# One block for the first attention and the search, tables among the key stores, key loads behind the first gathered rows, first scores as two, three, three

## The chip, the cores and the metric

The kernel runs on one core of a Trainium2 chip. The metric is the device time of one execution in microseconds (us); lower is better. A core has engines that run their own instruction streams and meet only at semaphores: TensorE (PE; its weight loads are shown as PEld), VectorE (DVE), ScalarE (ACT), GpSimd (POOL) and SyncE (SP), which here does nothing but start transfers. Transfers started by any of them run on the core's 16 DMA engines. In the profile an engine name with a q at its end (SPq, PEq, POOLq) is that engine's instruction queue: DMA starts, branches and barriers are put down to it.

## The reference

Two layers over x (16 batches, 112 tokens, width 256), each of them a cross attention to ctx (16 batches, 375 rows) and a feed-forward part. The first attention has no softmax; the first feed-forward is expert choice: each of 8 experts takes the 224 of the 1792 tokens with its highest gate scores. The second attention is an ordinary softmax attention with 16 heads, the second feed-forward a mixture with LoRA parts.

```python
# layer 0: x = x + attention(layernorm(x), ctx) without softmax, with its own layernorm
score = jnp.einsum('bhqd,bhkd->bhqk', Q, K) / dk
attn = jnp.where(mask, -jnp.inf, score)
...
# layer 0, feed-forward
k = int(bs * CAPACITY) // n
scores = jax.nn.softmax(xf @ gate_w.T, axis=-1)
vals, idx = jax.lax.top_k(scores.T, k)
...
h = jax.nn.gelu(h, approximate=True)
out = jnp.einsum('knf,ndf->knd', h, fc2s) + b2s
out = out * kept_w[..., None]
xf = xf.at[flat_idx].add(out.reshape(k * n, d))
...
# layer 1: x = x + softmax attention(layernorm(x), ctx), then the LoRA mixture
K = (key_value @ Wk.T + bk).reshape(B, SKV, H, Dh).transpose(0, 2, 1, 3)
weights = jax.nn.softmax(scores, axis=-1)
```

## The kernel before

The work is laid out in stages, each engine's part written as one function per block (`nc.Block`); a block ends with a barrier of all engines.

**Block 1, 0 to 170 us: the first attention.** It goes over 8 pairs of batches. The tail of a pair (`tail`, parts 0 to 6 on VectorE) adds the attention's result to x, normalises three times and gives `x1`, `xin` (the gate's input) and `z`. TensorE turns `xin` and multiplies it with the gate's weights (`gate_turn`, `gate_product`), ScalarE copies both (`gate_inputs`, `gate_logits`). GpSimd's `powers` raises the variances to -0.5 and, in its third step, adds `total` = x1 + xin. SyncE stores `z` to `gath_d`, from which the experts gather, and `total` to `sum_d`. Behind the last pair's products TensorE has already done 10 of 64 key pieces of the second attention (`key_piece`, L182; a piece is two matmuls on ctx and `wk1`, and a batch has four pieces).

**Block 2, 171.5 to 225 us: the gate and the search.** VectorE makes the softmax of the gate: the maximum (L872), `shifted` (L875), ScalarE's Exp into `raised` (L795), the sum (L878) and the scores. Then come 16 rounds (`bits`) that find for each expert the score that 224 tokens reach, two bits at a time: VectorE writes candidates and `above` (L920), TensorE counts (`tally`, L828), VectorE reduces the count (L925) and takes the bits. Between the tallies TensorE does the other key pieces, 3 or 4 in a round. Each batch's keys are kept as three bfloat16 parts in `kp`, which has KEPT = 5 slots: the first part is ScalarE's copy (L791, two for a batch), the whole value is `kf` (L798), the remainders `kr` are VectorE's `remainder(n)` (L895, one half, in round n, queued between `above` and the reduction of the count) and GpSimd's `second_half(n)` (L772), ScalarE copies them as second part (L807), GpSimd subtracts the third (L780). SyncE stores the three parts to `kparts_d` (L761), at most two stores under way; ScalarE waits for the store of batch n - 5 before it writes batch n. At the head of SyncE's part of the block stand three tables for the experts: `iota`, `b1` and `b2` (L753). In rounds 0 to 3 VectorE also splits the scores in three parts (`score_parts`, L901 to L910) for `find`.

After the last round VectorE writes `gt_eq_q` (L948) and, by way of two more products of TensorE, `pos1`, the place of each token in its expert's list. TensorE does values of the second attention in between (`value`, L730).

**Block 3, from 225 us: the experts.** For each expert `find` (one-hot rows against `token5`, L1070 and L1131) gives the indices, GpSimd gathers the expert's 224 rows of `gath_d` in two indirect transfers (L1038), TensorE turns them (L1141), multiplies (L1154 and, behind gelu, L1169) and GpSimd adds the weighted result to `sum_d` (L1047). The indices of expert e + 2 and their gathers are made during expert e. SyncE begins this block with the key loads of the first three batches (`load_keys`, L744: nine transfers from `kparts_d` to `kpk`) and then loads the weights `we` of experts 2 to 7, each when the expert two before is done (L997). Values of the second attention fill TensorE up to the first turn (L1141 at 241.3).

**Block 4, from 368 us: the second attention.** Statistics of x (`statistics`), `normal(i)` (L1888, VectorE), the turn of `xn` (L2047) and the queries (L2057) go pair by pair; their parts are copied as for the keys, with `remainder(i)` on VectorE (L1897). From pair 4 on TensorE does the scores of batch 0 in between (`score`, L2075, 8 groups, listed by pair in `FIRST_SCORES`), and VectorE takes their row maxima (`two_max`, L1920). `shift_turn(0)` (L2084) turns the maxima; ScalarE spreads the shift (L1809), TensorE forms the transposed scores (L2100), ScalarE their exponentials (`probs`, L1828). The stretch from there to about 600 us is 16 such steps; then the last feed-forward runs to the end.

## Time and profile before

| | us |
|---|---|
| median of 3 runs | 766.07 |
| lowest, highest | 765.29, 771.0 |
| the profiled execution | 770.76 |
| its span (first to last instruction) | 768.9 |
| mean granted TensorE clock, share of full | 0.978 |
| busy: TensorE, VectorE, ScalarE, GpSimd | 715.1, 501.3, 336.8, 293.9 |

The profile is taken from one execution. Its times count from the start of the span, so a row that begins with 171.52 starts 171.52 us into it. A group of instructions stands as one row: its start, the time from its first start to its last end, the engine, the line of the kernel, the operation, what it writes and reads, their shapes and how many instructions there are. In brackets at the end of a row stands how long the engine had been idle before it, and behind the arrow what ended this. PEclk is the clock that TensorE was granted, as a share of 2.4 GHz; at 0.50 it is 1.2 GHz.

### The profile page before, as it was taken

The page shows a single profiled execution, that of the slowest core. Times are in us where ns is not written, and L with a number is a line of the kernel's source. Part 1 is how long each engine was busy: PE and PEld are TensorE (multiplying, and loading weights), DVE is VectorE, ACT ScalarE, POOL GpSimd, SP SyncE. Part 2 cuts the span into 40 slices and gives each one's busy share as a digit, 9 for nine tenths or more (in the row PEclk, how much of TensorE's full clock was granted, in tenths as well). Part 3 has the DMA queues.
Part 4 walks back from the last instruction along what each step waited for, and adds up shares of the span by engine and source line. Part 5 has one row for each costly group of instructions (what it writes and reads, how often), then busy time and mean ns, then how long its engine had stood idle before and what let it go on. Part 6 is the DMA issues. An engine that isn't in the chain of part 4 may idle for free. (4 is left out here: it accounts for less than half of the span.)

```text
span 768.9 us, 16709 instructions
## 1 busy us (share of the span) xinstructions
PE 715.1 (93%) x6469; PEld 608.4 (79%) x6469; DVE 501.3 (65%) x1263; ACT 336.8 (44%) x689; POOL 293.9 (38%) x222
## 2 busy tenths in 40 slices
PE   4899999979988999999987999999998898999998
PEld 3678788855577989898875778777776787898998
DVE  4688888878862322320367787878788777767565
ACT  2112222218733221222546787777777642423323
POOL 2233333428841232232432877778778200000000
PEclk9999999999998999999998999999999999999999
DMA  9978000017889444543534588877762000000001
GB/s 295 336 225 50 25 25 25 26 49 206 196 176 159 133 147 134 147 164 89 108 94 92 115 149 164 172 150 155 148 142 37 2 2 13 1 25 1 25 5 34
DMA packets 65611, 81.55 MB, mean 106 GB/s; under 512 B 32018, under 2 KB 55154, under 8 KB 64226
## 3 DMA queue, kind: packets, MB, share of 16 engines
q1 hardware_dynamic: 62306, 72.22, 39.7%
q0 software_dynamic: 2816, 3.67, 2.7%
q10 hardware_dynamic: 416, 4.65, 1.6%
q8 instruction: 50, 0.82, 0.5%
q14 instruction: 23, 0.19, 0.1%
HBM read 60.45 MB, written 19.31 MB: 104 GB/s over the span
## 5 line engine op out<-in xcount | busy, mean ns | idle before, releaser
L1920 DVE TENSOR_REDUCE mx<-psum 112x2 f32<-112x750 f32 x128 | 113.2, 926 | 14.1 <-PE psum L2075 13.6
L1828 ACT ACTIVATE probs<-psum 125x448 f32<-125x448 f32 x192 | 91.1, 545 | 28.9 <-PE psum L2100 28.5
L574 PE MATMUL psum<-w_parts,c_parts 128*125 128x512 f32 x288 | 74.5, 412 | 11.0 <-DVE w_parts L437 10.6
L1735 POOL TENSOR_TENSOR half_sum<-probs 125x896 f32<-125x896 f32 x30 | 62.7, 2089 | 42.9 <-ACT probs L1828 42.8
L2100 PEld LDWEIGHTS psum<-qpk,kpk 128*125 128x125 bf16 x768 | 62.4, 141 | 15.3 <-issue 8.0
L574 PEld LDWEIGHTS psum<-w_parts,c_parts 128*125 128x125 f32 x288 | 54.2, 192 | 25.1 <-DVE w_parts L437 10.6
L2100 PE MATMUL psum<-qpk,kpk 128*125 128x112 bf16 x768 | 67.9, 227 | 2.6 <-ACT probs L1828 2.1
L2075 PE MATMUL psum<-kpk,qpk 96*112 96x375 bf16 x256 | 63.5, 342 | 6.3 <-DVE mx L1920 4.9
L1741 POOL TENSOR_TENSOR tile_sum<-half_sum,probs 125x896 f32<-125x896 f32 x30 | 62.5, 2084 | 3.4 <-issue 1.1
L1169 PE MATMUL psum<-we,hT 128*112 128x256 f32 x256 | 59.7, 394 | 0.0
L1014 ACT ACTIVATE hT<-psum,b 128x224 f32<-128x224 f32 x64 | 25.1, 443 | 78.8 <-PE psum L1154 78.8
L1440 ACT ACTIVATE ctx_all<-psum,cols 128x448 f32<-128x448 f32 (+1 forms) x40 | 22.4, 560 | 81.5 <-PE psum L1606 81.5
L1169 PEld LDWEIGHTS psum<-we,hT 128*112 128x112 f32 x256 | 46.9, 185 | 10.5
L1154 PE MATMUL psum<-rT,we 128*128 128x224 f32 x256 | 52.1, 364 | 0.9 <-ACT rT L1005 0.9
L1154 PEld LDWEIGHTS psum<-rT,we 128*128 128x128 f32 x256 | 50.2, 197 | 2.1 <-issue 1.2
L185 PE MATMUL psum<-ctx_all,wk 128*128 128x375 f32 x128 | 46.3, 504 | 3.6 <-PEq L264 3.5
L1101 DVE TENSOR_TENSOR tmp<-psum,b 112x512 f32<-112x512 f32 x8 | 5.5, 692 | 67.6 <-PE psum L1169 67.6
L2413 PE MATMUL psum<-wo_parts,hs_parts 128*112 128x256 f32 x384 | 48.1, 281 | 1.0 <-DVE hs_parts L2311 0.9
L2413 PEld LDWEIGHTS psum<-wo_parts,hs_parts 128*112 128x112 f32 x384 | 46.1, 175 | 1.9 <-DVE hs_parts L2311 1.6
L1047 POOL DMA_INDIRECT sum_d<-outs,idx_add x16 | 23.8, 1490 | 61.4 <-DVE outs L1105 37.0
L1412 POOL TENSOR_TENSOR rs<-ve,mhalf 112x4 f32<-112x4 f32 (+1 forms) x5 | 4.9, 975 | 109.2 <-DVE ve L1455 109.2
L1552 DVE SCALAR_TENSOR_TENSOR ctx_all<-psum,neg_bi,ctx_all 128x448 f32<-128x448 f32 (+1 forms) x40 | 23.5, 589 | 34.4 <-PE psum L1619 33.9
(234 smaller groups left out, 1498.7 us busy)
## 6 DMA issues: line engine op xcount, KB each, us to landing
we<-in_we SPq DMA_DIRECT2D x6, 2048.0 KB, 9.1
kparts_d<-kp SPq DMA_DIRECT2D x16, 562.5 KB, 5.3
kpk<-kparts_d SPq DMA_DIRECT2D x16, 562.5 KB, 6.2
ctx_all<-in_ctxT SPq DMA_DIRECT2D x16, 375.0 KB, 6.0
kpk<-kparts_d SPq DMA_DIRECT2D x16, 375.0 KB, 7.0
we<-in_we ACTq DMA_DIRECT2D x2, 2048.0 KB, 13.3
kpk<-kparts_d SPq DMA_DIRECT2D x16, 187.5 KB, 4.0
qparts_d<-qp SPq DMA_DIRECT2D x16, 168.0 KB, 3.1
```

The lines of the kernel that those rows point to most:

```text
L185: ins = pe.matmul(k_bank(n, m)[:, 0:SK], wk1[:, k, m * 128:(m + 1) * 128], ctx_of(n)[:, k], start=(k == 0), stop=(k == KC - 1))
L574: ins = pe.matmul(banks[B_KV[t]][0:KT, :], parts_of[:, x, k, t * KT:(t + 1) * KT], w_parts[:, k, w], start=(k == 0 and (x, w) == SPLIT[0]) ...
L1014: ins = act.activation(hT[:, s, f], banks[B_F[g]][:, (f % 2) * CAP:(f % 2 + 1) * CAP], ACT.Gelu_apprx_tanh, bias=b1[:, e, f:f + 1])
L1154: ins = pe.matmul(banks[B_F[g]][:, (f % 2) * CAP:(f % 2 + 1) * CAP], we1[:, s, k, f * 128:(f + 1) * 128], rT[:, s, k], start=(k == 0), sto ...
L1169: ins = pe.matmul(banks[B_OUT[s]][0:SQ, h * D:(h + 1) * D], hT[:, s, f, h * SQ:(h + 1) * SQ], we2[:, s, f], start=(f == 0), stop=(f == FC ...
L1735: pool.tensor_tensor(half_sum[:, m], probs[:, m, 0], probs[:, m, 1], ALU.add)\
L1741: pool.tensor_tensor(tile_sum[:, m], half_sum[:, m], probs[:, m, 2], ALU.add)\
L1828: act.activation(probs[:, m, t, g * HU * SQ:(g + 1) * HU * SQ], banks[B_ST[u % 3]][0:KT, 0:HU * SQ], ACT.Exp, scale=SCALE)\
L1920: dve.tensor_reduce(mx[:, n % 2, H + 2 * j:H + 2 * j + 2], psum[0:SQ, first:first + 2, 0:SK], AX.X, ALU.max)\
L2075: ins = pe.matmul(banks[B_S[j % 2] + h][0:SQ, 0:SK], qpk[0:ROWS, s, 2 * j + h], kpk[0:ROWS, s, 2 * j + h], start=True, stop=True)
L2100: ins = pe.matmul(banks[B_ST[u % 3]][0:KT, c * SQ:(c + 1) * SQ], kpk[:, s, h, t * KT:(t + 1) * KT], qpk[:, s, h], start=True, stop=True)
L2413: ins = pe.matmul(y_of(i, s), hs_parts[:, x, f, s * SQ:(s + 1) * SQ], wo_parts[:, w, f], start=(f == 0 and (x, w) == SPLIT[0]), stop=(f == ...
```

## The change

Four things are changed.

1. The functions of block 1 are written into block 2, so that the barrier between them goes. With it the order at the seam changes on each engine. VectorE makes the gate's maximum and `shifted` before the last pair's `z`, and `remainder(0)` moves into that pair's tail; `remainder(1)` and `(2)` come a round earlier and `remainder(15)` behind `gt_eq_q`. ScalarE copies the keys of batches 0 and 1 before the gate's input and logits. GpSimd's sum of the last pair moves behind the first tally. The four operations on the score parts leave VectorE: two are now ScalarE's copies, two GpSimd's subtractions. `shifted` and `raised` lie in PSUM.
2. The tables go among the key stores: `iota`, `b1` and half of `b2` behind the seventh store, the other half of `b2` behind the tenth.
3. SyncE's key loads wait until the rows of experts 0 and 1 have landed.
4. At the second attention's entry `FIRST_SCORES` is two, three, three; `normal` runs three pairs ahead, the statistics and the powers of all later pairs are done at pair 0, and `shift_turn(0)` waits for the last turned `xn` but one and not for the last query remainder.

The core of the diff (moved functions that are the same before and after are left out):

```diff
-FIRST_SCORES = {4: (0, 1), 5: (2, 3), 6: (4, 5), 7: (6, 7)}
+FIRST_SCORES = {4: (0, 1), 5: (2, 3, 4), 6: (5, 6, 7)}
...
-        with nc.Block() as block:
-            @block.sync
...
 (SyncE)
-        for dst, name in ((iota, "c_iota"), (b1, "b1"), (b2, "b2")):
-            sp.dma_start(dst[:], d[name]).then_inc(tabs_in.sem, 16)
+        sp.wait_ge(lg_done.sem, lg_done.at(PAIRS - 1))
         for n in range(B):
+            if n == 7:
+                for dst, name in ((iota, "c_iota"), (b1, "b1")):
+                    sp.dma_start(dst[:], d[name]).then_inc(tabs_in.sem, 16)
+            if n in (7, 10):
+                half = slice(0, E0 // 2) if n == 7 else slice(E0 // 2, E0)
+                sp.dma_start(b2[:, half], d["b2"][:, half]).then_inc(tabs_in.sem, 16)
...
 (ScalarE)
-                gate_inputs(PAIRS - 1)
-                gate_logits(PAIRS - 1)
-        first_part(0)
+        act.wait_ge(x1_done.sem, x1_done.at(PAIRS - 1))
+        first_parts(0)
+        whole(0)
+        first_parts(1)
+        gate_inputs(PAIRS - 1)
+        whole(1)
+        gate_logits(PAIRS - 1)
+        act.wait_ge(max_off.sem, max_off.at(0))
+        act.activation(raised[:], shifted[:], ACT.Exp).then_inc(exp_done.sem, 1)
+        act.wait_ge(z_done.sem, z_done.at(PAIRS - 1))
+        first_parts(2)
...
+            if n == 1:
+                act.wait_ge(count_done.sem, count_done.at(0))
+                act.activation(token5[:, :, 2], scores[:].rearrange("p b e -> p (b e)"), ACT.Copy)\
+                    .then_inc(parts_done.sem, 1)
+            if n == 6:
+                act.wait_ge(parts_done.sem, 2)
+                act.activation(token5[:, :, 3], rest[:], ACT.Copy).then_inc(parts_done.sem, 1)
...
 (GpSimd)
         second_half(0)
+        pool.wait_ge(count_done.sem, count_done.at(0))
         for n in range(B):
+            if n == 1:
+                sums(PAIRS - 1)
             if n + 1 < B:
                 second_half(n + 1)
...
+            if n == 3:
+                pool.wait_ge(parts_done.sem, 1)
+                pool.tensor_tensor(rest[:], scores[:].rearrange("p b e -> p (b e)"), token5[:, :, 2], ALU.subtract)\
+                    .then_inc(parts_done.sem, 1)
+            if n == 8:
+                pool.wait_ge(parts_done.sem, 3)
+                pool.tensor_tensor(token5[:, :, 4], rest[:], token5[:, :, 3], ALU.subtract).then_inc(parts_done.sem, 1)
...
 (VectorE)
+        for part in range(2 * NKT):
+            if part == 4:
+                remainder(0)
+            tail(part, PAIRS - 1, 1, more=False)
+
         route.step(0)
 
+        dve.wait_ge(lg_done.sem, lg_done.at(PAIRS - 1))
         dve.tensor_reduce(small[:, 0], logits[:], AX.X, ALU.max).then_inc(route.next(), 1)
         dve.memset(cur, 0.0)
         dve.wait_ge(route.sem, route.count())
         dve.tensor_tensor(shifted[:], logits[:], spread(small[:, 0], 2, E0), ALU.subtract)\
             .then_inc(max_off.sem, 1)
+        tail(2 * NKT, PAIRS - 1, 1, more=False)
...
+        remainder_at = lambda n: n - 1 if n < 3 else n
...
-            remainder(r)
-            score_parts(r)
+            for n in range(1, B - 1):
+                if remainder_at(n) == r:
+                    remainder(n)
...
         ins.then_inc(gt_eq_q_done.sem, 1)
+        remainder(B - 1)
...
 (the experts' block, SyncE, then TensorE)
+        for s in range(2):
+            sp.wait_ge(gathered[s].sem, gathered[s].at(0))
         for b in range(AHEAD):
             for r in (3, 2, 1):
                 load_keys(sp, b, r)
...
+        pe.wait_ge(parts_done.sem, 4)
         find(0, 0)
...
 (the second attention: GpSimd, VectorE, TensorE)
-            if i + STATS_AHEAD < PAIRS:
-                power(i + STATS_AHEAD)
+            if i == 0:
+                for later in range(STATS_AHEAD, PAIRS):
+                    power(later)
...
-            if i + 2 < PAIRS:
-                normal(i + 2)
+            if i + 3 < PAIRS:
+                normal(i + 3)
+            scored = FIRST_SCORES.get(i, ())
+            ahead = int(len(scored) > 2)
+            for j in scored[:ahead]:
+                two_max(0, j)
             remainder(i)
-            if i + STATS_AHEAD < PAIRS:
-                statistics(i + STATS_AHEAD)
-            for j in FIRST_SCORES.get(i, ()):
+            if i == 0:
+                for later in range(STATS_AHEAD, PAIRS):
+                    statistics(later)
+            for j in scored[ahead:]:
                 two_max(0, j)
...
-        pe.wait_ge(qr_done.sem, qr_done.at(PAIRS - 1))
+        pe.wait_ge(xnT_done.sem, xnT_done.at(PAIRS - 2))
         shift_turn(0)
         for j in range(2):
             score(1, j)
+        pe.wait_ge(qr_done.sem, qr_done.at(PAIRS - 1))
```

The next rows are VectorE's instructions in order, from the last pair's third variance to the sum of the softmax; first before, then after the change. A row has the line, the operation, the tile written and those read, the shape, and the semaphores it waits for.

```order
L483 TENSOR_SCALAR ve<-mv 112x2 [waits stats]
L533 SCALAR_TENSOR_TENSOR t<-xin,mv,rows 112x256 x2
L543 SCALAR_TENSOR_TENSOR z<-t,rs,rows 112x256 [waits z_out,rstd_done,stats]
L543 SCALAR_TENSOR_TENSOR z<-t,rs,rows 112x256
L264 UNCONDITIONAL_BRANCH
L867 UNCONDITIONAL_BRANCH [waits barrier_Pool_Activation_PE_DVE_SP_release]
L872 TENSOR_REDUCE small<-logits 112x16
L873 MEMSET psum 112x8
L875 TENSOR_TENSOR shifted<-logits,small 112x128 [waits route]
L878 TENSOR_REDUCE small<-raised 112x16 [waits exp_done]
```

```order
L669 TENSOR_SCALAR ve<-mv 112x2 [waits stats]
L727 SCALAR_TENSOR_TENSOR t<-xin,mv,rows 112x256 x2
L761 TENSOR_REDUCE small<-logits 112x16 [waits lg_done]
L762 MEMSET psum 112x8
L764 TENSOR_TENSOR psum<-logits,small 112x128 [waits route]
L737 SCALAR_TENSOR_TENSOR z<-t,rs,rows 112x256 [waits z_out,rstd_done,stats]
L737 SCALAR_TENSOR_TENSOR z<-t,rs,rows 112x256
L768 TENSOR_REDUCE small<-psum 112x16 [waits exp_done]
```

The branches of the block's end and the wait for the barrier are gone, and the maximum and the subtraction stand ahead of the two `z` operations, behind which the Exp's result is waited for.

SyncE's order in the search and at the head of the experts' block, after the change (`k_out0` and `k_out1` are the landings of earlier stores, `gathered0` and `gathered1` those of the first two experts' rows). Before it, the three tables `iota`, `b` (`b1`) and `b` (`b2`, 112x2048 in one) stood ahead of the first store.

```order
L412 DMA kparts_d<-kp 128x6x375 [waits k3_done,k_out0,k2_done,k1_done]
L402 DMA iota<-in_c_iota 112x224
L402 DMA b<-in_b 128x64
L405 DMA b<-in_b 112x1024
L412 DMA kparts_d<-kp 128x6x375 [waits k3_done,k_out1,k2_done,k1_done]
L412 DMA kparts_d<-kp 128x6x375 [waits k3_done,k_out0,k2_done,k1_done]
L412 DMA kparts_d<-kp 128x6x375 [waits k3_done,k_out1,k2_done,k1_done]
L405 DMA b<-in_b 112x1024
...
L1004 UNCONDITIONAL_BRANCH [waits k_out1,k_out0]
L356 DMA kpk<-kparts_d 48x2x3000 [waits gathered1,gathered0]
```

Four transfers now stand between stores that wait for one another, and the first key load has a wait of its own.

TensorE's order from the scores behind pair 5's queries to the first shift turn, before and after (L2057 and L2082 are the queries, L2075 and L2100 the scores, two rows for one group; L2084 and L2109 the turn of the maxima).

```order
L2075 MATMUL psum<-kpk,qpk 112x375 [waits max_done]
L2075 MATMUL psum<-kpk,qpk 112x375
L2057 MATMUL psum<-xnT,wq 128x224 [waits qr_done,xnT_done]
L2057 MATMUL psum<-xnT,wq 128x224 x3
L2075 MATMUL psum<-kpk,qpk 112x375 [waits max_done]
L2075 MATMUL psum<-kpk,qpk 112x375
L2075 MATMUL psum<-kpk,qpk 112x375 [waits max_done]
L2075 MATMUL psum<-kpk,qpk 112x375
L2084 MATMUL psum<-ident,mx 32x112 [waits max_done,qr_done]
```

```order
L2100 MATMUL psum<-kpk,qpk 112x375 [waits max_done]
L2100 MATMUL psum<-kpk,qpk 112x375
L2100 MATMUL psum<-kpk,qpk 112x375 [waits max_done]
L2100 MATMUL psum<-kpk,qpk 112x375
L2082 MATMUL psum<-xnT,wq 128x224 [waits qr_done,xnT_done]
L2082 MATMUL psum<-xnT,wq 128x224 x3
L2109 MATMUL psum<-ident,mx 32x112 [waits max_done,xnT_done]
```

The last pair's queries are no longer followed by two groups of scores, and the turn behind them waits for `xnT_done` where it waited for `qr_done`.

## Rows read from the trace of the kernel before

**Rows 1.** The page, part 1: busy us (share of the span) and instructions.

```profile
PE 715.1 (93%) x6469; PEld 608.4 (79%) x6469; DVE 501.3 (65%) x1263; ACT 336.8 (44%) x689; POOL 293.9 (38%) x222
```

**Rows 2.** Windows: span, busy us by engine, then PEclk, DMA share, GB/s.

```profile
190.00:200.00 10.00, 10.00 (x48) 5.85 (x48) 8.24 (x29) 8.12 (x16) 8.72 (x9) 1.00 0.84 193
200.00:210.00 10.00, 10.00 (x50) 5.90 (x48) 7.93 (x28) 7.34 (x14) 8.68 (x7) 1.00 0.77 187
210.00:220.00 10.00, 8.86 (x67) 6.77 (x66) 5.62 (x20) 5.42 (x9) 6.30 (x6) 1.00 0.98 225
310.00:320.00 10.00, 10.00 (x65) 8.78 (x64) 2.93 (x17) 2.90 (x7) 3.97 (x4) 0.83 0.63 206
```

**Rows 3.** The timeline at the block boundary: start, us, engine, line, operation.

```profile
156.12 0.87 DVE L543 SCALAR_TENSOR_TENSOR z<-t,rs,rows 112x256 f32<-112x256 f32 x2
...
168.11 1.25 POOL L385 TENSOR_TENSOR total<-x,xin 112x512 f32<-112x512 f32 x1
168.20 0.18 ACT L345 ACTIVATE logits<-psum 112x16 f32<-112x16 f32 x1 [1.04 <-PE psum L639]
168.23 1.82 DVE L543 SCALAR_TENSOR_TENSOR z<-t,rs,rows 112x256 f32<-112x256 f32 x2 [0.25 <-DVE t L533]
...
171.52 0.29 DVE L872 TENSOR_REDUCE small<-logits 112x16 f32<-112x128 f32 x1 [1.47 <-PEq L264]
...
172.51 0.29 DVE L878 TENSOR_REDUCE small<-raised 112x16 f32<-112x128 f32 x1 [0.37 <-ACT raised L795]
...
174.30 0.31 PE L828 MATMUL psum<-above,ones 112*128 112x32 bf16 x4
...
174.71 3.45 PE L185 MATMUL psum<-ctx_all,wk 128*128 128x375 f32 x8
...
185.31 2.76 PE L185 MATMUL psum<-ctx_all,wk 128*128 128x375 f32 x8
```

**Rows 4.** The timeline of TensorE before and in the first experts.

```profile
231.39 7.15 PE L730 MATMUL psum<-wv,ctx_all 128*125 128x256 f32 x32
241.29 1.01 PE L1141 MATMUL psum<-ident,rows 112*128 112x112 f32 x4 [2.74 <-DMA rows<-gath_d,idx]
243.19 8.54 PE L1154 MATMUL psum<-rT,we 128*128 128x224 f32 x32 [0.90 <-ACT rT L1005]
...
268.24 0.58 PE L1141 MATMUL psum<-ident,rows 112*128 112x112 f32 x4
...
275.56 6.22 PE L1154 MATMUL psum<-rT,we 128*128 128x224 f32 x32
```

**Rows 5.** Waits in 395 to 420 us, before and in the first scores.

```profile
PE psum L2047 <- DVE xn L1888: 3.7, 2, 2.2
```

**Rows 6.** The timeline at the first shift and first probabilities.

```profile
417.94 0.54 PE L2084 MATMUL psum<-ident,mx 112*32 112x112 f32 x4 [1.97 <-DVE mx L1920]
...
421.64 2.37 ACT L1828 ACTIVATE probs<-psum 125x448 f32<-125x448 f32 x5
```

**Rows 7.** The timeline at the last round of the search.

```profile
212.37 0.34 PE L828 MATMUL psum<-above,ones 112*128 112x96 bf16 x4 [0.34 <-DVE above L920]
...
213.32 0.61 DVE L895 SCALAR_TENSOR_TENSOR kr<-psum,cols,kp 128x375 f32<-128x375 f32 x1 [1.00 <-POOL kp L780]
...
213.84 0.26 DVE L925 TENSOR_REDUCE psum<-psum 112x24 f32<-112x96 f32 x1
```

**Rows 8.** Issues in 170 to 262 us: KB of one, us to landing.

```profile
kparts_d<-kp SPq DMA_DIRECT2D x16, 562.5 KB, 5.3
...
b<-in_b SPq DMA_DIRECT2D x1, 896.0 KB
```

**Rows 9.** Issues in 228 to 230 us: key loads and a gather.

```profile
kpk<-kparts_d SPq DMA_DIRECT2D x1, 562.5 KB, 18.4
...
rows<-gath_d,idx POOLq DMA_INDIRECT x2, 12.4
```

**Rows 10.** Issues in 254 to 257 us: two gathers, no key load.

```profile
rows<-gath_d,idx POOLq DMA_INDIRECT x2, 2.8
```

879 lines of the change are left out of this document (430 added, 449 removed).

## The prediction

> **What bounds the kernel now.** I read four views in this order. The page first: TensorE is busy 93% of the span [rows 1], so a gain has to come out of the 7% in which it idles, or out of stretches in which it runs at half clock. The busy shares by window next: in the search (190 to 210 us) TensorE is full, VectorE has 8 of 10 us and GpSimd 8.7, and the DMA engines are at 0.84 and 0.77, then 0.98 in 210 to 220 [rows 2]. That stretch is a chain over five engines, not TensorE alone. Then the timeline around the three places that the change touches. At the block boundary VectorE has the gate's logits at 168.38 (168.20 + 0.18) and first looks at them at 171.52 [rows 3]. Before the first expert TensorE ends its values at 238.54 (231.39 + 7.15), idles 2.74 us for gathered rows, and then runs the turn and the first product slowly: 1.01 and 8.54 us, where the same groups take 0.58 and 6.22 later [rows 4]. Before the first scores of the second attention it idles 3.7 us in two waits for `xn` and 1.97 us for the last row maximum [rows 5, 6]. The expert loop behind it keeps TensorE full, 10.00 of 10 in the window shown [rows 2], so what is saved before it arrives at its end.
>
> **Part A, one block.** The barrier goes, and VectorE runs the maximum and `shifted` ahead of `z`, so that ScalarE's Exp lies under `z`. VectorE can start the maximum at 168.40. From the start of the maximum to the first tally took 2.78 us (171.52 to 174.30), 0.37 of it waiting for Exp [rows 3]. Add `z` at its normal 0.87 and take the 0.37 out: the tally comes at 168.40 + 2.78 + 0.87 - 0.37 = 171.68, or 2.6 us earlier. `z` took 1.82 before, beside GpSimd's sum of 1.25; another pair's took 0.87 [rows 3], and the change moves this sum behind the first tally. That is the 0.95 in the gain that has least to do with the barrier; if `z` stays slow the gain is 1.6. The upper bound is from the clock: eight key matmuls took 3.45 us at 174.71, after the idle at the barrier, and 2.76 at 185.31 [rows 3]. TensorE now has key pieces to do where it stood idle, and if its clock stays at 2.4 GHz, 0.7 more is saved, together 3.3. I take 2.6. The copies of the first two batches' keys and remainder(0) move ahead into waits for GpSimd and cost nothing: TensorE's order has the pieces that they need ahead of the last pair's turn, as before.
>
> The GpSimd half that now runs at 168.14 stands beside `shifted`. The Trainium skill, "SBUF — State Buffer", in its single rule on contention says that a VectorE instruction with two SBUF inputs and a GpSimd one reading SBUF exclude each other for the whole instruction; by that `shifted` would start some 0.3 us late and the term would be 2.3. The doubled `z` beside the sum agrees with it.
>
> **Part A, the last round.** VectorE waited 1.00 us for GpSimd, then ran a remainder of 0.61, and reduced at 213.84 a count that TensorE had begun at 212.37 and ended at 212.71 [rows 7]. The remainder is now behind `gt_eq_q`. The reduction could start at about 212.85: 1.0 us. The four score-part operations leave VectorE too, but in rounds that TensorE or the chain bounds; nothing for them. Two of them and the sum are new on GpSimd, which has 1.3 us free in ten [rows 2]: 1.25 for the sum and between 0.2 and 1.25 for each subtraction, some 2 to 3 us in a search of 40. They can make the keys late, not the tallies, until a kept buffer is missing.
>
> **Part B, tables among the stores.** 896 KB [rows 8] and 81 KB of small tables leave the stretch in which no store was waiting, and go among the stores behind the seventh and tenth (about 193 and 203 us before). At the 193 to 225 GB/s of those windows they take 4.3 to 5.1 us of the DMA engines, say 4.7. Idle there between 193.6 and 210 is 0.16 x 6.4 + 0.23 x 10 = 3.3 us [rows 2]; the 1.4 left over goes into 210 to 220, where the share is 0.98, so the late stores slip by it. A store frees one of five buffers, ScalarE's next copy waits for it, VectorE's remainder for that, and the count's reduction is queued behind the remainder. I take 1.3 given back; below it nothing (the rounds have their own slack), above it all 4.7. **A and B: 2.6 + 1.0 - 1.3 = 2.3 us**, between -1.1 (1.6 + 1.0 - 3.7, where one us of the 4.7 falls in the rounds' slack) and 4.3.
>
> **Part C, key loads behind the first rows.** Nine key loads (3.4 MB) went out at 225 and the gathers were issued among them. A gather landed 12.4 us later [rows 9]; with no key load beside it one takes 2.8 [rows 10]. Expert 0's second gather left at 228.56 and landed at 241.3, when the turn began. Now it leaves with the engines free: 228.56 - 2.3 + 2.8 = 229.1, expert 1's at about 234.1, and the values end at 236.2. The wait goes: 2.74. With it the half clock should go, since TensorE idles only the 0.90 for `rT`: 1.01 - 0.58 = 0.43 and 8.54 - 6.22 = 2.32 [rows 4]. **C: 5.5 us.** If the clock falls anyway, 2.7. What is late next: SyncE issues the key loads from 234.1 on, they end about 20 us later (one took 18.4 [rows 9]), so near 254. The gathers of expert 2, at 254 to 256 before, now leave near 246.7 and 248, beside them. At 12.4 us they land at 260.4 at the latest; the turn that needs them was at 268.24 [rows 4] and comes at 260.4. So the margin is nought by that figure and several us if the last key load's end sets it. Keys themselves aren't needed before 400.
>
> The Trainium skill, "DMA: Bandwidth & Descriptors", section "Queues, rings and completion order", speaks against this part: each DMA engine takes turns between queue rows, packet by packet. GpSimd's gather has a row of its own, so beside one queue of key loads it would take about twice 2.8, 5.6 us, and land before the values end with or without the change; C would be nothing. The 12.4 us doesn't agree with that.
>
> **Part D, entry of the second attention.** `normal` goes one pair further ahead, maxima come two, three, three, the first shift turns after them and no longer after the last query remainder. Waits of 3.7 for `xn` and 1.97 at the turn can go [rows 5, 6]. But the first probabilities, at 421.64, stand at the end of ScalarE's chain (query parts of the last pair, table load, values, spread), and that chain keeps its work; it starts earlier only as the last pair's queries do. The five pairs' copies still alternate between TensorE, ScalarE and VectorE. **I take 1.0**, between 0 and the whole 5.7, nearer to 0, as the ScalarE chain isn't shortened.
>
> **Sum.** 2.3 + 5.5 + 1.0 = 8.8 us, that is 770.76 - 8.8 = 762.0 against the profiled execution (span 768.9, 1.9 around it). That execution lies 4.7 above the median of the runs shown, 766.07. The gain is in waits that each execution has, so the median goes to 766.07 - 8.8 = 757.3; half-clock spells fall differently in other executions, and I say 757.5. One per cent (7.66 us) is about what a measurement of this kernel can tell from no change; 758.4 is that bound.
>
> **Rivals.**
> 1. The clock falls again between values and first expert (it fell under the same low activity before). C is 2.7, the sum 6.0: 760.1. Chance 0.17.
> 2. The stores give the search's gain back whole (GpSimd and DMA both near full for it, the extra slack of TensorE's rounds against): A and B are 0: 6.5 stay, 759.6. At the lower end, 1.1 lost, it is 760.7. Chance 0.13.
> 3. C doesn't do what it says: late key loads hold expert 2's gathers or the expert weights behind them on SyncE's queue, or the gather was slow from something else. 8.8 - 5.5 = 3.3: 762.8. For it speaks the margin of nought, against it that all key loads are out by 254. Chance 0.10.
> 4. The scores' order pays all of D's waits (5.7) and no other term changes: 13.5, 752.6. Chance 0.12.
> 5. Slower than before: the half clock. Two of the eight experts had a spell in the find and turn, where the matmuls are small though TensorE is full; each cost 10 x (1 - 0.83) = 1.7 us [rows 2]. With the loop 8 us earlier all eight could be hit: 6 x 1.7 = 10.2, more than 8.8: 767.5. It decides from five further spells on. Against it: six of eight passed before. Chance 0.05.
>
> The forecast has the remaining 0.43, with a range of its own of 755.5 to 760. Faster by over 1%: most of it and rival 4, 0.5. Within 1%: 0.45. Slower: 0.05. The range 752.5 to 764 leaves out rival 5, and the worst of 2 and 3 together.
>
> **What would show it.** Tally at 171.7 or earlier, `z` 0.87; reduction of the last round right behind its tally; first find near 221.4. No TensorE wait for rows before the first turn, products of 6.2 us, rows landing in about 3 us. Expert loop 7 to 8 us earlier, its end too. First probabilities at 412.5 to 413. I would be wrong if ScalarE's waits for stores grow beyond 1.5 us each, if the turn of expert 2 waits for rows, or if more than two spells of half clock stand in the expert loop.

## The result

Measured side by side with the kernel before, the changed kernel takes 765.93 us (median of 20 runs, 762.98 to 767.69) against 768.85 (20 runs, 765.29 to 771.37). The ratio is 0.9967, with a 95% interval of 0.9952 to 0.9983: 2.5 us or 0.3% faster, where 8.6 us (757.5, range 752.5 to 764) was forecast. The base of the forecast, 766.07, was the median of three runs; twenty runs of the same kernel gave 768.85, so 2.8 of the 8.4 us between 757.5 and 765.93 lie in the base and not in what the change did. The profiled executions differ by 3.2 us: 765.7 us of span against 768.9. Most of what is missing was given back in three places that the sum didn't contain: the values ahead of the experts, the choice of the tokens, and the expert loop.

The page of the changed kernel, part 1 and the span (columns as in [rows 1]):

```profile
span 765.7 us, 16706 instructions
...
PE 715.2 (93%) x6469; PEld 608.3 (79%) x6469; DVE 500.9 (65%) x1259; ACT 337.8 (44%) x691; POOL 294.9 (39%) x224
```

TensorE's busy time is the same to 0.1 us (715.1 in [rows 1]); the half clock stretches busy time, so this alone doesn't show what it did. The timeline of the changed kernel at the place where the barrier was, which answers to [rows 3]:

```profile
166.36 2.13 DVE L727 SCALAR_TENSOR_TENSOR t<-xin,mv,rows 112x256 f32<-112x256 f32 x2
...
167.37 0.84 POOL L574 TENSOR_TENSOR kr<-kf,kp 128x375 f32<-128x375 f32 x1
...
168.41 0.27 DVE L761 TENSOR_REDUCE small<-logits 112x16 f32<-112x128 f32 x1
...
168.93 0.87 DVE L737 SCALAR_TENSOR_TENSOR z<-t,rs,rows 112x256 f32<-112x256 f32 x2
...
169.72 0.28 DVE L768 TENSOR_REDUCE small<-psum 112x16 f32<-112x128 f32 x1
...
171.49 0.25 PE L950 MATMUL psum<-above,ones 112*128 112x32 bf16 x4 [2.27 <-DVE above L789]
...
171.59 4.46 PE L185 MATMUL psum<-ctx_all,wk 128*128 128x375 f32 x8
```

`z` is back at 0.87, as forecast, and the sum starts 1.31 us behind the maximum's start. But now the `t` operations before it take 2.13 us and not 0.88 as in the kernel before:

```profile
167.10 0.88 DVE L533 SCALAR_TENSOR_TENSOR t<-xin,mv,rows 112x256 f32<-112x256 f32 x2
```

The first key remainder of GpSimd (0.84) lies beside them, where `powers` and then the sum stood before. The first tally is at 171.49, 2.8 us earlier; 0.75 of this came up in the first 82 us, which the change doesn't touch, so the part's own share is 2.06. Behind it eight key matmuls take 4.46 us where they took 3.45 [rows 3]: the clock falls later here, to 1.2 GHz about 0.9 us behind the start of the first tally (granted clock 1.00 in 171.49 to 172.40, 0.51 in 172.40 to 175.89).

The last round and the choice of the tokens, which answer to [rows 7]:

```profile
210.68 0.34 PE L950 MATMUL psum<-above,ones 112*128 112x96 bf16 x4 [0.65 <-DVE above L789]
...
211.06 0.27 DVE L795 TENSOR_REDUCE psum<-psum 112x24 f32<-112x96 f32 x1 [0.44 <-PE psum L950]
...
214.18 3.14 POOL L585 TENSOR_TENSOR kp<-kr,kp 128x750 bf16<-128x750 f32 x2
...
214.62 1.28 DVE L832 TENSOR_TENSOR tie<-tie,gt_eq_q 112x128 f32<-112x128 f32 x1
...
215.93 1.54 DVE L834 TENSOR_TENSOR taken<-tie,gt_eq_q 112x128 bf16<-112x128 f32 x1
```

The reduction now starts 0.38 behind its tally, 1.47 before; that is the microsecond that the moved remainder was to bring. Then `tie` and `taken` take 1.28 and 1.54 us beside two key parts of GpSimd (3.14 together). In the trace of the kernel before they took 0.29 each, since they came after GpSimd had ended (214.24 + 3.08 = 217.32); only `need` ahead of them took 0.55 there, 0.17 here. These are the rows of the kernel before:

```profile
214.24 3.08 POOL L780 TENSOR_TENSOR kp<-kr,kp 128x750 bf16<-128x750 f32 x2
...
217.70 0.29 DVE L962 TENSOR_TENSOR tie<-tie,gt_eq_q 112x128 f32<-112x128 f32 x1
218.03 0.29 DVE L964 TENSOR_TENSOR taken<-tie,gt_eq_q 112x128 bf16<-112x128 f32 x1
```

The first experts, which answer to [rows 4], and the gathers, which answer to [rows 9, 10]:

```profile
230.07 8.84 PE L342 MATMUL psum<-wv,ctx_all 128*125 128x256 f32 x32
238.74 0.55 PE L1158 MATMUL psum<-ident,rows 112*128 112x112 f32 x4
240.44 6.29 PE L1171 MATMUL psum<-rT,we 128*128 128x224 f32 x32 [1.15 <-ACT rT L1022]
```

```profile
rows<-gath_d,idx POOLq DMA_INDIRECT x2, 2.9
```

The gather lands in 2.9 us (12.4 before), there is no wait ahead of the turn, and the first product takes 6.29 (8.54 before). But the values ahead of it take 8.84 where they took 7.15: TensorE runs at half clock there for 3.4 us. Windows over the values, before and after (columns as in [rows 2]):

```profile
231.39:238.54 7.15, 7.15 (x35) 5.91 (x34) 4.09 (x22) 1.62 (x2) 2.01 (x2) 1.00 1.02 164
```

```profile
230.07:238.74 8.67, 8.67 (x35) 7.20 (x34) 3.90 (x22) 1.62 (x2) 2.07 (x2) 0.80 0.42 93
```

Of the 2.74 that the wait was worth, 1.7 went into this.

The expert loop, by windows (columns as in [rows 2]); the last figure but two is the clock:

```profile
290.00:300.00 10.00, 10.00 (x65) 8.66 (x64) 2.07 (x12) 2.42 (x6) 3.58 (x3) 0.83 0.55 181
310.00:320.00 10.00, 10.00 (x59) 8.36 (x59) 0.56 (x4) 1.30 (x3) 2.09 (x2) 0.83 0.29 72
330.00:340.00 10.00, 10.00 (x44) 8.36 (x43) 1.44 (x6) 0.54 (x1) 2.09 (x2) 0.86 0.14 36
```

Three spells of half clock, where the kernel before has two; each falls while TensorE is full, at the turn behind the find products. The entry of the second attention, which answers to [rows 6]:

```profile
410.69 0.54 PE L2109 MATMUL psum<-ident,mx 112*32 112x112 f32 x4 [0.45 <-DVE mx L1940]
...
412.53 1.28 ACT L1870 ACT_TABLE_LOAD   x1
...
416.25 1.50 PE L2125 MATMUL psum<-qpk,kpk 128*125 128x112 bf16 x12 [4.24 <-ACT qpk L1828]
417.44 2.37 ACT L1847 ACTIVATE probs<-psum 125x448 f32<-125x448 f32 x5
```

The first turn is 7.3 us earlier than before and waits only 0.45; then TensorE waits 4.24 for `qpk`, because ScalarE's chain from the last query part and the table load (412.53) to the spread is what it was (from the table load to the first exponentials 4.91 us, as before).

The whole account, from landmark to landmark on TensorE (starts of groups: the gate's turn of the last pair, the first tally, the gt_eq products, the taken products, the first experts' turns, the values behind the loop, the first transposed scores, the last matmul), each the difference of two starts in the timeline:

| stretch | before | after | difference | forecast |
|---|---|---|---|---|
| start to the gate's turn | 165.98 | 165.23 | -0.75 | 0 |
| to the first tally | 8.32 | 6.26 | -2.06 | -2.6 |
| to gt_eq | 41.01 | 41.16 | +0.15 | +0.3 |
| to taken | 3.58 | 4.87 | +1.29 | 0 |
| to the turn of expert 0 | 22.40 | 21.22 | -1.18 | -2.7 |
| to the turn of expert 2 | 26.95 | 24.50 | -2.45 | -2.75 |
| to the values behind the loop | 99.99 | 101.61 | +1.62 | 0 |
| to the first transposed scores | 52.24 | 51.40 | -0.84 | -1.0 |
| to the end | 345.38 | 346.33 | +0.95 | 0 |
| sum | 765.85 | 762.58 | -3.27 | -8.8 |

The first line is variation and not gain: over all the kernels traced here the stretch to the gate's turn takes 163.59 to 165.98 us, and the kernel before has the longest. The last two stretches together are 397.62 before and 397.73 after, so in this pair of traces nothing of the gain at the first scores reaches the end.

### The profile page after: what moved, and what is told of

The parts are those of the page before. It is cut to its first block and busy times, and to the rows that moved or that the text cites. A ratio compares the mean times of both kernels' runs of the same rounds, so it can differ in the third digit from the quotient of the medians.

```text
span 765.7 us, 16706 instructions
## 1 busy us (share of the span) xinstructions
PE 715.2 (93%) x6469; PEld 608.3 (79%) x6469; DVE 500.9 (65%) x1259; ACT 337.8 (44%) x691; POOL 294.9 (39%) x224
## 5 line engine op out<-in xcount | busy, mean ns | idle before, releaser
L1940 DVE TENSOR_REDUCE mx<-psum 112x2 f32<-112x750 f32 x128 | 113.3, 925 | 13.7 <-PE psum L2100 13.0
L2125 PEld LDWEIGHTS psum<-qpk,kpk 128*125 128x125 bf16 x768 | 62.6, 142 | 18.6 <-issue 11.3
L2100 PE MATMUL psum<-kpk,qpk 96*112 96x375 bf16 x256 | 63.1, 338 | 7.2 <-DVE mx L1940 5.7
L1171 PE MATMUL psum<-rT,we 128*128 128x224 f32 x256 | 49.8, 353 | 1.2 <-ACT rT L1022 1.2
L1171 PEld LDWEIGHTS psum<-rT,we 128*128 128x128 f32 x256 | 48.4, 190 | 1.8 <-ACT ctx_all L351 1.3
```

The costliest lines, as they stand in the source:

```text
L1171: ins = pe.matmul(banks[B_F[g]][:, (f % 2) * CAP:(f % 2 + 1) * CAP], we1[:, s, k, f * 128:(f + 1) * 128], rT[:, s, k], start=(k == 0), sto ...
L1940: dve.tensor_reduce(mx[:, n % 2, H + 2 * j:H + 2 * j + 2], psum[0:SQ, first:first + 2, 0:SK], AX.X, ALU.max)\
L2100: ins = pe.matmul(banks[B_S[j % 2] + h][0:SQ, 0:SK], qpk[0:ROWS, s, 2 * j + h], kpk[0:ROWS, s, 2 * j + h], start=True, stop=True)
L2125: ins = pe.matmul(banks[B_ST[u % 3]][0:KT, c * SQ:(c + 1) * SQ], kpk[:, s, h, t * KT:(t + 1) * KT], qpk[:, s, h], start=True, stop=True)
```

## The experiments

All of them were timed in five rounds beside the kernel before. The ratio is to the kernel before; the changed kernel's is 0.9967. A difference of two such ratios is uncertain by about 0.3%, some 2 us, so the stretches of the traces carry more of the argument than the medians do. Each kernel was timed beside runs of the kernel before of its own (their medians are 767.68 to 768.74), and the ratio comes from these and not from the first line of the table; each row's stretches are those of one execution. "First key piece" in two of the expectations means a landmark 11.9 us ahead of the gate's turn; 18.2 and 17.0 from there are 6.3 and 5.1 from the turn.

| kernel | median us | ratio (95%) | turn to tally | to gt_eq | to taken | to turn 0 | to turn 2 | loop | half clock in loop |
|---|---|---|---|---|---|---|---|---|---|
| before | 768.85 | 1 | 8.32 | 41.01 | 3.58 | 22.40 | 26.95 | 99.99 | 6.8 |
| after | 765.93 | 0.9967 (0.9952 to 0.9983) | 6.26 | 41.16 | 4.87 | 21.22 | 24.50 | 101.61 | 10.2 |
| u_keys | 767.49 | 0.9983 (0.9954 to 1.0011) | 6.25 | 40.84 | 4.58 | 22.17 | 24.30 | 99.97 | 6.8 |
| u_scores | 769.37 | 1.0006 (0.9979 to 1.0033) | 6.26 | 40.80 | 5.05 | 21.21 | 24.50 | 99.98 | 6.8 |
| u_tables | 766.57 | 0.9978 (0.9952 to 1.0004) | 6.25 | 43.66 | 3.91 | 19.53 | 24.50 | 101.66 | 10.2 |
| a_only | 771.31 | 1.0033 (1.0008 to 1.0058) | 6.25 | 44.27 | 3.91 | 21.50 | 24.30 | 103.36 | 13.7 |
| c_before | 766.82 | 0.9997 (0.9967 to 1.0027) | 8.32 | 41.01 | 3.58 | 21.18 | 24.50 | 101.65 | 10.2 |
| d_before | 766.96 | 0.9988 (0.9968 to 1.0008) | 8.32 | 41.20 | 3.58 | 22.10 | 24.30 | 99.94 | 6.8 |
| late_parts | 764.26 | 0.9936 (0.9914 to 0.9957) | 6.26 | 41.04 | 3.54 | 20.69 | 24.50 | 103.28 | 13.7 |
| half_z | 764.37 | 0.9945 (0.9924 to 0.9967) | 5.54 | 40.62 | 5.03 | 19.53 | 24.50 | 101.70 | 10.2 |
| ports | 764.85 | 0.9950 (0.9928 to 0.9972) | 5.53 | 42.64 | 3.54 | 20.69 | 24.50 | 101.67 | 10.2 |
| spread2 | 760.39 | 0.9892 (0.9859 to 0.9925) | 6.26 | 42.63 | 4.64 | 21.21 | 23.03 | 96.26 | 0 |
| b_spread2 | 762.94 | 0.9914 (0.9882 to 0.9946) | 8.32 | 40.60 | 3.58 | 22.73 | 22.82 | 96.26 | 0 |
| nokeys_spread2 | 762.48 | 0.9924 (0.9894 to 0.9954) | 6.27 | 41.85 | 5.10 | 21.94 | 25.59 | 96.26 | 0 |
| ports_spread2 | 758.96 | 0.9873 (0.9841 to 0.9906) | 5.53 | 42.68 | 3.54 | 21.66 | 23.02 | 96.26 | 0 |
| b2_late | 764.70 | 0.9954 (0.9926 to 0.9981) | 6.26 | 40.02 | 3.91 | 19.54 | 24.50 | 98.31 | 3.4 |
| best | 759.56 | 0.9876 (0.9837 to 0.9915) | 5.53 | 40.21 | 3.54 | 19.84 | 23.72 | 96.31 | 0 |

**Part C taken out of the changed kernel** (u_keys): SyncE's two waits ahead of the key loads are deleted.

```diff
     def _(sp):
-        for s in range(2):
-            sp.wait_ge(gathered[s].sem, gathered[s].at(0))
         for b in range(AHEAD):
```

> The changed kernel with the key loads put back: they go out at the head of the experts' block with no wait for rows. Theory 1, the waits add up as forecast: the gather takes 11 to 12 us again, TensorE waits about 2.7 us before the first turn and runs the first product at half clock, so the time is 5.5 us longer than the changed kernel's. Theory 2, the half clock only moves: the wait of 2.7 comes back, but one of the spells later in the expert loop (there were three, one of 3.4 us in the values before it) goes, so it is 1.5 to 4 us longer. Theory 3, the loads were hidden: no difference, rows landing in under 4 us.

Measured: 0.9983, 1.2 us above the changed kernel, with an interval that reaches below it. In the trace the turn waits only 0.79 us for the rows and the first product stays at full clock:

```profile
227.80 8.84 PE L342 MATMUL psum<-wv,ctx_all 128*125 128x256 f32 x32
237.43 0.60 PE L1156 MATMUL psum<-ident,rows 112*128 112x112 f32 x4 [0.79 <-DMA rows<-gath_d,idx]
238.93 6.29 PE L1169 MATMUL psum<-rT,we 128*128 128x224 f32 x32 [0.90 <-ACT rT L1020]
```

The values ran partly at half clock here too (8.84), so TensorE came to the turn later and found the rows nearly there. Both stretches to the turn of expert 2 together are 0.75 us longer than in the changed kernel, and the loop, with two spells and not three, 1.64 shorter. Theory 1 (5.5 us) falls, theory 2 is nearest.

**Part C alone, on the kernel before** (c_before): the same two waits added there.

> The kernel before with the key loads behind the first rows, nothing else. Theory of the forecast: the rows' wait of 2.74 and the half clock behind it (2.75) go, 5.5 us. Clock theory: the wait goes, from the values' end to the first turn nothing is idle, but the half-clock time comes back elsewhere in the values or in the expert loop, so 1 to 4 us in all; from the product before the turn to expert 1's first product the trace shows the whole 5.5, and from there to the end of the loop 1.7 or 3.4 more than the 103.3 us of two spells.

Measured: 0.9997. From taken to the turn of expert 2 it takes 45.68 us against 49.35, so 3.7 of the 5.5 come, the rest is eaten by the half clock in the values (8.84 again), and the loop gives back 1.66 with a third spell. 2.0 us are left in the trace; the median, 0.2 us, can't tell this from nothing.

**The block and the tables.** u_tables puts all tables in front of the first key store:

```diff
         for n in range(B):
-            if n == 7:
+            if n == 0:
                 for dst, name in ((iota, "c_iota"), (b1, "b1")):
                     sp.dma_start(dst[:], d[name]).then_inc(tabs_in.sem, 16)
-            if n in (7, 10):
+            if n == 0:
+              for half in (slice(0, E0 // 2), slice(E0 // 2, E0)):
+                sp.dma_start(b2[:, half], d["b2"][:, half]).then_inc(tabs_in.sem, 16)
+            if n == 99:
                 half = slice(0, E0 // 2) if n == 7 else slice(E0 // 2, E0)
                 sp.dma_start(b2[:, half], d["b2"][:, half]).then_inc(tabs_in.sem, 16)
```

The loads under `n == 99` never run.

> The changed kernel with all tables in front of the first key store. Theory 1: the stores at the end of the search come up to 1.4 us earlier, ScalarE's waits for stores (0.9, 0.5, 1.3 and 1.9 us) shrink, tallies 14 and 15 come 0.5 to 1 us earlier and the whole is 0 to 1 us shorter. Rival: the tables hold up stores 0 to 2 instead, and the time is 0 to 1 us longer. If neither shows in the tallies the tables' place costs nothing.

a_only has this, the two waits of the key loads out, and the old entry of the second attention.

> The merged block alone: key loads, tables and the scores' entry as in the kernel before. Theory 1: 2 to 3.5 us shorter than the kernel before, as the tally is 2.8 us earlier and the last round 1 us shorter. Theory of the shared port: the first tally is 2 to 3 us earlier, but GpSimd's last key parts lie beside VectorE's tie and taken (0.29 us each alone, 1.28 and 1.54 in the changed kernel), so the first find is only 0.5 to 1.5 us earlier, and the time 0 to 1.5 us shorter.

Measured: 0.9978 and 1.0033. The merged block alone is slower than the kernel before. Its first tally comes 2.07 us earlier, as in the changed kernel, but the search takes 44.27 us for 41.01 (43.66 in u_tables, 41.16 with the tables among the stores). The waits in the search, first a_only, then the changed kernel:

```profile
ACT kp L480 <- DMA kparts_d<-kp: 9.0, 5, 6.9
```

```profile
ACT kp L477 <- DMA kparts_d<-kp: 4.6, 4, 1.9
```

With the tables ahead, ScalarE waits once 6.9 us for a key store to land (4.5 in u_tables), and VectorE's remainder and the round's count with it. So in the search the tables' place isn't a cost of 1.3 us beside the merged block; it spares 2.5 to 3.1 us that the merged block would else have lost. That is more than the search varies by with the tables among the stores: 40.62 to 42.68 us in the ten traces that have all of them there. But it doesn't reach the experts: u_tables is at the turn of expert 2 97.85 us behind the gate's turn, the changed kernel 98.01, since the values of u_tables ran at full clock (7.15). The theory of the shared port held in kind but not in place: the search ends later here, `tie` and `taken` lie clear of GpSimd at 0.29 each, and `need`, a small operation of 0.17 us with one input, takes 1.44 beside the key parts and ends with them; taken comes after 3.91 us.

```profile
214.71 3.25 POOL L588 TENSOR_TENSOR kp<-kr,kp 128x750 bf16<-128x750 f32 x2
216.55 1.44 DVE L828 TENSOR_SCALAR need<-need 112x8 f32<-112x8 f32 x1
```

The search alone doesn't make a_only slower: from the gate's turn to the turn of expert 2 it takes 100.24 us, the kernel before 102.26. The 2.0 us are lost again in the loop, with four spells for two (103.36 us for 99.99). The stretch from the values behind the loop to the last matmul, which a_only leaves as it was, takes 400.72 us for 397.62, with 10 us more of half clock than the changed kernel or the one before; that is the whole of its 3.1 us (772.0 to 768.9), it is luck, and the median's 2.5 is the better figure. Both of my expectations for u_tables missed the search by 2.5 us.

**The entry of the second attention.** u_scores puts it back in the changed kernel, d_before puts the new one into the kernel before; the edit is that of the last part of the diff.

> The changed kernel with the entry of the second attention put back (scores two, two, two, two, normal two pairs ahead, shift turn behind the last query remainder). Theory 1: the ScalarE chain bounds the first probabilities, 0 to 1 us longer than the changed kernel's. Rival: the whole of the 3.7 and 2.0 us of TensorE's waits counts, 3 to 5 us longer. In the changed kernel's trace the first turn is 7.3 us earlier than before and the first probabilities 4.2, with 3.4 of this from the stages before; so 0.8 by that.

> The kernel before with the new entry of the second attention alone. Theory of the forecast, ScalarE's chain bounds the first probabilities: from the end of the expert loop to the first transposed scores 53.0 to 53.5 us (54.2 before), 0.5 to 1.5 us shorter in all. Rival: the whole of TensorE's waits counts, 3 to 5 us shorter; taking it out of the changed kernel cost 3 us in the median but 1.4 in the trace.

Measured: 1.0006 and 0.9988. In the traces the stretch from the loop to the first transposed scores is 52.80 in u_scores against 51.40, and 51.22 in d_before against 52.24. So the part is worth 1.0 to 1.4 us, by the kernel before 0.9 us in the median. The 3.0 us between the medians of u_scores and the changed kernel are more than that; with an interval of 2 us it is no contradiction, and the trace decides for the ScalarE chain. The traces of the other kernels bear it out at the first transposed scores: 52.17 to 53.11 us with the old entry (five kernels), 50.62 to 52.16 with the new one (thirteen). Whether it reaches the end isn't as clear. Among the traces with the same 13.7 us of half clock behind the loop, loop to last matmul takes 397.62 to 399.59 with the old entry (four) and 397.42 to 398.58 with the new (eight).

**GpSimd's key parts beside VectorE.** late_parts and half_z add one wait each, ports has both:

```diff
+        pool.wait_ge(z_done.sem, z_done.at(PAIRS - 1))
         second_half(0)
...
                 second_half(n + 1)
+            if n == B - 2:
+                pool.wait_ge(taken_done.sem, taken_done.at(0))
             pool.wait_ge(k2_done.sem, k2_done.at(n))
```

> The changed kernel, with GpSimd's third key parts of the last two batches waiting until VectorE has written taken. Shared port theory: tie and taken take 0.29 us each again (1.28 and 1.54 in the changed kernel), the taken products start 3.6 us behind the gt_eq product as in the kernel before (4.9 in the changed one), 1.3 us gained at the first find, and 1 to 1.5 us in the time if no spell of half clock falls otherwise. Rival, the two operations are slow because of their own operands: no change in them.

> The changed kernel, with GpSimd's first key remainder waiting for the last z. Shared port theory: the two t operations take 0.88 us together again (2.13 in the changed kernel), the first tally comes 1.2 us earlier, counted from the first key piece 17.0 us and not 18.2, and the time is 0.5 to 1.2 us shorter. Rival: the remainder now lies beside the scores operations of the gate and delays these by as much: no change at the first tally.

> Both of GpSimd's waits of the last runs together in the changed kernel: the first key remainder behind z, the last two third parts behind taken. Shared port theory: first tally 17.5 us behind the first key piece (18.2), taken 3.55 us behind the gt_eq product (4.87), so 2 us at the first find; the median 1 to 2.5 us shorter than the changed kernel's, not more than the sum of the two (0.9936 and 0.9945 of the kernel before, against 0.9967). If the two medians were luck of the half clock, it stays at 0.995 or above.

Measured: 0.9936, 0.9945 and 0.9950. The timeline of late_parts, then of half_z:

```profile
213.48 0.29 DVE L834 TENSOR_TENSOR tie<-tie,gt_eq_q 112x128 f32<-112x128 f32 x1
...
213.81 0.29 DVE L836 TENSOR_TENSOR taken<-tie,gt_eq_q 112x128 bf16<-112x128 f32 x1
214.18 3.09 POOL L587 TENSOR_TENSOR kp<-kr,kp 128x750 bf16<-128x750 f32 x2 [1.32 <-DVE taken L836]
```

```profile
165.94 0.87 DVE L728 SCALAR_TENSOR_TENSOR t<-xin,mv,rows 112x256 f32<-112x256 f32 x2
...
168.73 0.85 POOL L574 TENSOR_TENSOR kr<-kf,kp 128x375 f32<-128x375 f32 x1 [1.76 <-DVE z L738]
```

With GpSimd elsewhere, `tie` and `taken` take 0.29 us and the `t` pair 0.87, as in the kernel before (0.29 and 0.88). So the mechanism is shown at both places: an instruction of GpSimd on SBUF beside one of VectorE with both inputs in SBUF. The Trainium skill ("SBUF — State Buffer", section "Who interferes with whom") has it that the later of two such instructions waits for the whole of the earlier; 1.28 us for an operation of 0.29 that began 0.44 into a GpSimd instruction of about 1.57 agrees (0.44 + 1.28 = 1.72, so it ends 0.15 behind the end of GpSimd's first). The order of the starts doesn't agree for `t`: its second operation starts at 166.8, takes 1.74 us and ends 0.28 behind GpSimd's remainder, which starts after it, at 167.37. What it was worth in time: the first wait 1.3 us at taken, the second 0.7 at the tally (1.2 was expected; 0.4 of the rest is the wait for the logits, which now ends last). The medians gained 2.4 and 1.7 us, with intervals that overlap the changed kernel's by a little; together they gained only 1.3. The reason stands in the search of ports: 42.64 us. Its rounds 12 to 15 took 2.97, 4.04, 3.29 and 3.07 us (2.14, 2.78, 2.14 and 2.65 before). An earlier start meets the key stores; that fits, but it isn't shown alone. Ports ran its first round in 2.70 us, at full clock, where the changed kernel took 4.40. The changed kernel's own search does the same in spread2, with 2.71 in the first round and 42.63 in all, while half_z, with the start of ports, took 40.62. So a fast first round is in part lost again in the last ones, and by how much varies by 2 us from trace to trace.

**b2 out of the search** (b2_late): its two halves go between the gathers' wait and the key loads, VectorE waits for them ahead of the first bias. best has this, both GpSimd waits and the find products spread as below.

> The changed kernel with the table b2 (896 KB) loaded behind the first rows and ahead of the key loads, not among the key stores. Store theory: rounds 12 to 15 of the search take 2.1 to 2.8 us each whatever the start, ScalarE's waits for stores in the search go from 4.6 to under 2.5 us, 0.5 to 1.5 us shorter than the changed kernel. Rival, the stores alone fill the queue: late rounds as before, no difference; or b2 delays the key loads and expert 2's gathers: 1 to 3 us longer.

> All that has helped together: both GpSimd waits, find products spread, b2 behind the first rows. Store theory: the earlier first tally now reaches the first find, 1 to 2.5 us shorter than the kernel with the first two (0.9873): 0.984 to 0.986. If b2 was not what held the late rounds: 0.987.

Measured: 0.9954 and 0.9876. The search of b2_late is 40.02 us, 1.1 less than the changed kernel's, and that of best 40.21 against 42.68 of ports_spread2. But rounds 14 and 15 are still 2.69 and 3.12 (b2_late) and 2.69 and 3.03 (best), and ScalarE waits for stores 5.5 and 5.9 us in all. So b2 was a part of it; that the sixteen key stores themselves hold the last rounds is what is left, and isn't shown. In the median b2_late gains 1.0 us within an interval of 2, best nothing over ports_spread2; both traces are of the fastest run of their kernel (760.14 and 755.89). Whether a sixth kept buffer would clear it wasn't tried.

**The half clock in the expert loop.** The first try, spread, cut each expert's 32 find products into four groups of eight behind the quarters of the first expert product.

> The changed kernel, with each expert's 32 find products (5 columns wide) cut into four groups of eight, one behind each quarter of the first expert product, where they stood in one row of 32 behind it. Clock theory: the half clock in the expert loop comes from the stretch of find and turn; cut up, the three spells of 3.4 us there go, 1.7 us each, so about 5 us in the trace and 3 to 5 us in the median. Rival: the spells come from somewhere else or move: as many spells, time as the changed kernel's within 1 us.

Measured: 792.47 us, 1.0313. The find products were now ahead of the one-hot rows that VectorE makes:

```profile
260.69 0.58 PE L1150 MATMUL psum<-token,onehot 112*112 112x5 bf16 x8 [3.46 <-DVE onehot L1087]
```

Waits of this kind, 18.6 us in five, are a new bound. The half clock came back behind them: 20.5 us of it in the loop, in four places, each right behind such a wait. So the try doesn't tell whether the find products in one row were the cause, but half clock came behind every one of these waits. spread2 has them in the second product:

```diff
-            if more:
-                find(i + 1, s)
             if turn_next:
                 turn(i + s, 1 - s)
...
                     ins = pe.matmul(banks[B_OUT[s]][0:SQ, h * D:(h + 1) * D],
                                     hT[:, s, f, h * SQ:(h + 1) * SQ], we2[:, s, f],
                                     start=(f == 0), stop=(f == FC - 1))
+                    if more and h == 0 and f % 2:
+                        find(i + 1, s, (f // 2,))
```

> The changed kernel, with each expert's 32 find products in four groups of eight behind each quarter of the first half of the second expert product. The first try at this put them into the first product, where TensorE waited 3.5 us in each expert for the one-hot rows of VectorE; here they are needed later and the rows have 8 us more. Clock theory: the three spells of 3.4 us in the expert loop go, from expert 1's first product to the loop's end 99.9 us and not 104.9, 3 to 5 us shorter in the median than the changed kernel. Rival: spells stay or move (104 to 106.6 us), or the interleaving costs TensorE as much.

> The kernel before with its find products in four groups among the second expert product. Clock theory: the two spells in its expert loop go as the three in the changed kernel did (103.3 us to 98 us), 3 to 6 us shorter than the kernel before. Rival: the gain needs the change (its earlier gathers): under 2 us.

> The changed kernel with find products spread, and the key loads back at the head of the experts' block without a wait. Against spread2 (0.9892) this is the worth of the key loads' wait where no spell can come back in the expert loop. Forecast's theory: 5.5 us, 0.996. Clock theory: only TensorE's idle time for the rows, about 1.5 to 2 us (that segment took 7.0 us without and 5.5 with the wait), 0.991 to 0.992.

> The kernel of the two GpSimd waits and of the find products among the second expert product. If both theories hold, the gains add: 0.988 to 0.991 of the kernel before, 759.5 to 762 us. If the half clock only moves, the same as with the two waits alone.

Measured: 0.9892, 0.9914, 0.9924 and 0.9873. The same windows as above, in spread2:

```profile
290.00:300.00 10.00, 10.00 (x76) 8.91 (x75) 2.74 (x15) 2.80 (x7) 2.51 (x3) 1.00 0.54 184
310.00:320.00 10.00, 10.00 (x67) 8.79 (x66) 2.75 (x13) 0.79 (x2) 2.84 (x3) 1.00 0.31 70
330.00:340.00 10.00, 10.00 (x55) 9.30 (x54) 1.45 (x5) 3.58 (x9) 4.82 (x4) 1.00 0.71 235
```

No spell is left in the loop, in any of the five kernels that have it, and the loop takes 96.3 us. The other kernels fall on steps by the number of spells: 98.31 with one (b2_late), 99.94 to 99.99 with two (four kernels), 101.61 to 101.70 with three (five), 103.28 and 103.36 with four. A spell of 3.4 us costs 1.67 us, none would be 96.6 by these steps, and the number of them is no property of the change: late_parts has four, where the changed kernel has three, with nothing altered in the loop. That is what the forecast's sum took for granted, a loop that hands on what is saved ahead of it. b_spread2 gains 0.9% on the kernel before without anything of the change, so the spells were worth more than the whole change. The spell in the values isn't touched by this. In spread2, b_spread2 and ports_spread2 it is there as before (8.78 and twice 8.84 us), and in all nine kernels whose values took over 8.7 us it begins within 0.6 us of the end of expert 1's find products, which are still in one row; cutting these up wasn't tried.

nokeys_spread2 shows what the key loads' wait does when nothing else can move. In its trace the values ran at full clock (7.15), and the wait and the half clock behind it are back as they were before the change:

```profile
229.73 7.15 PE L342 MATMUL psum<-wv,ctx_all 128*125 128x256 f32 x32
239.12 1.01 PE L1159 MATMUL psum<-ident,rows 112*128 112x112 f32 x4 [2.25 <-DMA rows<-gath_d,idx]
241.03 8.65 PE L1172 MATMUL psum<-rT,we 128*128 128x224 f32 x32 [0.90 <-ACT rT L1020]
```

Against spread2 that is 0.32% or 2.5 us in the median, and 3.3 by the traces from taken to the turn of expert 2 (47.53 against 44.24). That lies nearer to the clock theory's 1.5 to 2 than to the forecast's 5.5; with intervals of 0.3% each, the median alone wouldn't tell it from nothing. The fastest kernels are ports_spread2 and best, 1.3% and 1.2% under the kernel before; the two can't be told apart.

## Why the prediction missed

**What held.** The barrier, `z` clear of the sum, and Exp under `z`: the first tally came 2.06 us earlier (2.6 forecast). The last round's reduction right behind its tally. Gathers in 2.9 us, no wait ahead of the first turn, the first product at full clock. The first scores: TensorE's waits for `xn` down from 4.0 to 1.1 us, the turn's from 1.97 to 0.45, little of it at the first transposed scores, 0.84 for 1.0. The key loads behind the rows didn't hold up expert 2: its gathers landed in 8.1 us and TensorE never waited.

**What didn't.** Two of the three signs of being wrong came: ScalarE waited 1.9 us for a store, and three spells stood in the loop. The first find was at 222.43 (221.4 forecast), the turn of expert 2 came 5.0 us earlier and the loop's end 3.4 (7 to 8), the first probabilities at 417.44 (412.5 to 413).

**Step 1 that failed: "so what is saved before it arrives at its end".** The loop's own time isn't fixed. It took 1.62 us more, a third spell. Rival 5 had the mechanism and the price of a spell (1.7) right, but let it matter only from five further ones on (at 1.7 these cost 8.5 of the 8.8); one was enough to take a fifth of the gain, and I gave the forecast no allowance for it.

**Step 2: the 5.5 us of part C.** The rows' wait was 2.74 and the half clock behind it 2.75, and both did vanish where I had put them. But the half clock fell in the values ahead of the turn instead, 1.7 us. u_keys and d_before, which keep the early key loads, have this spell in the values too, and there the wait for the rows shrinks, in u_keys to 0.79: the rows land when they land, and TensorE spends the time either slow or idle. So most of C's worth was one and the same time counted as two terms. The 5.5 was also the largest of several draws: with the early key loads, taken to the turn of expert 2 takes 49.35 us in the kernel before, but 46.40 in d_before, 46.47 in u_keys and 45.80 in a_only; with the wait it is 44.03 to 45.72 in the eight kernels whose find products stand in one row. Two kernels with the same spell in the values, c_before and d_before, differ by 0.7 us; two without it, u_tables and a_only, by 1.8, a_only's wait for the rows. Rival 1 named a clock that falls again between values and first expert at 2.7 for C; part of that came.

**Step 3: "nothing" between gt_eq and taken.** Moving the remainder brought the 1.0 us, and brought `tie` and `taken` forward into GpSimd's last key parts; 1.29 lost. The row that would have told it is the doubled `z` beside the sum [rows 3], which I used for `shifted` alone, by the rule of the Trainium skill ("SBUF — State Buffer"), at 0.3 us. The collision I had to look for was at every VectorE operation with two inputs in SBUF that the change moves in time: `t` lost 1.25, `tie` and `taken` 2.24.

**Step 4: the sign of part B.** I had it at 1.3 us given back against the search before; measured, the search is 0.15 longer, with 1.0 gained and the slower first round (4.40 for 3.70) in it, so about 0.5 was given back in rounds 14 and 15. The size was off by little. But B's worth is seen against the merged block without it, which a_only shows 3.3 us slower in the search than the kernel before. I had reckoned the merged block's stores as if the tables could still be out of the way.

What stays open: the 0.95 us between the first transposed scores and the end. Traces with the same 13.7 us at half clock behind the loop range from 345.38 to 347.12 there, with and without the new scores' order, so it is within what this stretch varies by, and no cause was found. Nor is it known why the loop has one spell in one trace and four in another.

## What to carry to other kernels

Ahead of a stretch in which TensorE is full, a gain isn't banked: the clock fell in this one from one to four times with nothing altered in the loop's own work, so count its half-clock rows in several executions and remove their cause before small shifts ahead of them are judged. When an operation is moved to another time, list what the other of VectorE and GpSimd does at the new time, above all for operations with two inputs in SBUF. A wait and the half clock behind it are one stall; price them as one, and ask how much of it slower work ahead would already fill.
